# Gathering with an add into the output's place, and experts four tiles of keys earlier

## The chip, the cores and the metric

One core of a Trainium2 chip runs the kernel. The metric is the device time of one execution in microseconds (us), as the median of several runs. Lower is better.

## The reference

The input x holds 2 sequences of 2048 tokens of 128 numbers, 4096 tokens in all. Everything is float32. With xn = layernorm(x) the result is

```
s      = xn W_spin^T + b_spin
local  = softmax((s W_J^T) s^T / sqrt(128)) s        # per sequence, 2048 x 2048
attn   = tanh(beta * (s + mean(s) W_global^T + local))
logits = xn Wg^T + bg ; the two best of 16 experts, softmax over the two
moe    = sum over the two of weight * (gated(xn Wgu[e] + bgu[e]) Wd[e] + bd[e])
out    = x + attn + moe
```

Each token goes through exactly 2 of 16 experts, so the expert part works on 8192 (token, expert) pairs.

## The kernel before, in words

**Attention.** The 4096 tokens are split into 8 query blocks (k, `NSB`) of 512. Each block walks over the 16 key tiles (j, `TB`) of its sequence, which gives 128 steps i = 16k + j (`STEPS`). In a step TensorE makes the scores of one key tile against the block's 512 queries (`score`, 3 products of 128x128 by 128x512, lines 556 to 558, for a value is kept as a high and a low part), ScalarE takes the exponential (L921) and the high part (L932, `ph`), VectorE the low part (L1106, `pl`), and TensorE multiplies both with the key tile's rows (`values`, 3 products at the same lines) two steps later (`LAG`). The block that comes next needs a row of maxima before its first step: 16 products (`maxima`, L609), each reduced on VectorE (L1121), spread over the steps j = 0 to 11 of the block before (`maxima_at`), then `shifts` at j = 12 and `shift_row` at j = 13. After a block its sum is turned (`fields`, L717 and L718, in steps 16k + 24 and 16k + 26), divided (`combine`, L1142 and L1145) and squashed (`squash`, L959) into `field`.

**Routing and scatters.** VectorE and GpSimd work out for every token which slot of the expert list each of its two pairs has (`choose`, and `route` in pieces 4 to 12; `ROUTE_AT` says in which step a piece stands). When the first positions `posu` are there, GpSimd issues 64 indirect DMAs (L517, one for each of 32 token tiles and each of the two choices), which scatter token rows of 512 B into the DRAM table `slots_x`.

**Experts.** The steps stop at step `MOE_AT` = 76 and the experts' part takes the engines: 20 groups of 4 slot tiles are read from `slots_x` into `xy`, turned (`turn_slots`, L661; the first two groups in steps MOE_AT - 2 and MOE_AT - 1), multiplied (`gate_up`, `down`), and stored as 1 KB rows (high and low half) into the DRAM table `slots_y`. The scores of steps 76 to 79 are made inside this part. Its turned tiles use the PSUM banks of the maxima, so the maxima of the steps before have to be reduced first.

**The end.** After the last `slots_y` store GpSimd issues 64 indirect gathers (L547): for each block k of 4 token tiles 4 gathers of the first choice into `made` and 4 of the second into `gy`. VectorE, between its attention work, adds `gy` to `made` (`add_both`, L1279, 1024 elements a partition), adds the two halves (`add_parts`, L1284, 512), and adds `field` (`finish`, L1290, 512). The tokens x themselves are loaded by SyncE (`tokens_in`) into `xs` and added to `field` by VectorE (`add_x`, L1275, 512). SyncE stores the finished block. `made` has room for 4 blocks and `gy` for 2. For the last block the adds stand at the end of VectorE's program (L1397 to L1410), ahead of `combine(7, ...)`.

The order on every engine is written out by hand: each engine runs its list in order and waits on semaphores.

## Time and profile before

| | us |
|---|---|
| median of 3 runs | 362.93 (360.56 to 363.42) |
| profiled execution, own time | 362.15 |
| profiled execution, span from first to last instruction | 360.4 |
| TensorE busy in the span | 324.9 (90%) |
| VectorE busy | 309.9 (86%) |
| ScalarE busy | 256.8 (71%) |
| GpSimd busy | 203.7 (57%) |

The times of the rows below are microseconds from the start of the span. The profiled execution's own time is 1.75 us longer than its span. Matmuls overlap in the records: one of 512 columns is listed with 0.39 us, but the next begins 0.2265 us later when nothing holds it up. So TensorE's real work is counted in products and not in busy time.

### The profile page before, as it was taken

What the parts mean: (1) busy time and instruction counts of PE and PEld (TensorE: products, weight loads), DVE (VectorE), ACT (ScalarE), POOL (GpSimd) and SP (SyncE); (2) the same over time, 40 slices, a digit from 0 to 9 for tenths busy, and PEclk for the clock granted to TensorE, in tenths of its full rate; (3) what the DMA queues carried; (4) which work ended last, traced back from release to release, by engine and by line L of the source; (5) the groups of instructions that cost most, each with busy time, mean ns of one, the idle gap of its engine ahead of it and who ended that gap; (6) DMA issues with size and microseconds to landing.
All of it is one profiled execution on the core that took longest, in us unless ns stands there. A gap on an engine that the chain in (4) does not pass through costs nothing.

```text
span 360.4 us, 5972 instructions
## 1 busy us (share of the span) xinstructions
PE 324.9 (90%) x1778; PEld 271.9 (75%) x1779; DVE 309.9 (86%) x630; ACT 256.8 (71%) x509; POOL 203.7 (57%) x271
## 2 busy tenths in 40 slices
PE   1878999998999999999978999999899998989980
PEld 1666788776777778888768999999788786867750
DVE  5988979999978999999769999888878999987855
ACT  2754777876699797687646988888787586578751
POOL 4276851325777777777113444534137777777760
PEclk9978999999999999999999999999999999999996
DMA  5999710000111211212222877765543354555551
GB/s 148 325 332 340 282 35 0 1 31 7 51 51 54 80 46 53 90 51 82 74 87 75 241 222 229 235 207 178 178 117 107 104 164 123 131 145 133 133 126 34
DMA packets 41359, 45.97 MB, mean 128 GB/s; under 512 B 3770, under 2 KB 33082, under 8 KB 41330
## 3 DMA queue, kind: packets, MB, share of 16 engines
q1 hardware_dynamic: 36162, 32.94, 29.1%
q0 software_dynamic: 5168, 12.67, 12.4%
q8 instruction: 15, 0.25, 0.3%
q14 instruction: 14, 0.11, 0.1%
HBM read 23.46 MB, written 22.12 MB: 126 GB/s over the span
## 4 chain that ended last, share of the span: by engine, by line
PE 40%; DVE 22%; POOL 19%; issue 8%; ACT 5%; DMA 4%; POOLq 0%; SPq 0%; ACTq 0%; DVEq 0%
POOL made L547 9%; POOL gy L547 8%; PE PS L556 8%; PE PS L558 8%; PE PS L557 8%; DVE mx L1121 6%; DVE pl L1106 5%; PE PS L609 4%; PE PS L661 2%; PE PS L786 2%; PE PS L771 2%; DVE stats L1077 2%; DMA xy<-slots_x 1%; PE PS L788 1%; PE PS L791 1%
## 5 line engine op out<-in xcount | busy, mean ns | idle before, releaser
L921 ACT ACTIVATE PS<-PS 128x512 f32<-128x512 f32 x128 | 74.8, 585 | 42.8 <-PE PS L558 41.2
L1106 DVE TENSOR_TENSOR pl<-PS,ph 128x512 fp32r<-128x512 f32 x128 | 87.7, 685 | 14.1 <-ACT ph L932 13.5
L1121 DVE TENSOR_REDUCE mx<-PS 128x1 f32<-128x512 f32 x128 | 84.3, 682 | 6.0 <-PE PS L609 6.0
L932 ACT ACTIVATE ph<-PS 128x512 fp32r<-128x512 f32 x128 | 76.5, 598 | 12.1 <-PE PS L558 0.8
L517 POOL DMA_INDIRECT slots_x<-xn,posu x64 | 63.0, 985 | 19.7 <-issue 17.1
L609 PE MATMUL PS<-xT,gq 128*128 128x512 f32 x128 | 49.5, 423 | 6.6 <-DVE mx L1121 6.3
L556 PE MATMUL PS<-gq,xT 128*128 128x512 f32 x128 | 52.4, 410 | 1.5 <-ACT gq L937 0.8
L556 PE MATMUL PS<-ph,rows 128*128 128x512 f32 x128 | 51.5, 402 | 1.8 <-DVE pl L1106 1.8
L558 PE MATMUL PS<-gq,xT 128*128 128x512 f32 x128 | 50.1, 391 | 0.0
L558 PE MATMUL PS<-ph,rows 128*128 128x512 f32 x128 | 50.1, 391 | 0.0
L557 PE MATMUL PS<-pl,rows 128*128 128x512 f32 x128 | 50.0, 391 | 0.0
L557 PE MATMUL PS<-gq,xT 128*128 128x512 f32 x128 | 50.0, 390 | 0.0
L536 POOL TENSOR_TENSOR gu_sb<-gu_sb 128x512 f32<-128x512 f32 x20 | 25.9, 1293 | 40.9 <-DVE gu_sb L1353 40.9
L547 POOL DMA_INDIRECT made<-slots_y,posu x32 | 32.2, 1007 | 20.0 <-DMA slots_y<-yr 10.6
L609 PEld LDWEIGHTS PS<-xT,gq 128*128 128x128 f32 x128 | 24.5, 194 | 18.1 <-DVE mx L1121 13.2
L547 POOL DMA_INDIRECT gy<-slots_y,posu x32 | 32.2, 1006 | 9.8 <-issue 9.8
L556 PEld LDWEIGHTS PS<-ph,rows 128*128 128x128 f32 x128 | 24.1, 188 | 8.8 <-DVE pl L1106 4.7
L556 PEld LDWEIGHTS PS<-gq,xT 128*128 128x128 f32 x128 | 24.1, 189 | 6.0 <-DVE pl L1106 1.0
L1026 ACT ACTIVATE yr<-PS,w_slot 128x256 f32<-128x256 f32 x72 | 28.2, 488 | 0.0
L558 PEld LDWEIGHTS PS<-ph,rows 128*128 128x128 f32 x128 | 24.0, 188 | 5.3
L558 PEld LDWEIGHTS PS<-gq,xT 128*128 128x128 f32 x128 | 24.0, 188 | 5.3
L557 PEld LDWEIGHTS PS<-pl,rows 128*128 128x128 f32 x128 | 24.1, 188 | 4.4
(199 smaller groups left out, 682.8 us busy)
## 6 DMA issues: line engine op xcount, KB each, us to landing
slots_y<-yr SPq DMA_DIRECT2D x20, 512.0 KB, 3.1
slots_x<-xs SPq DMA_DIRECT2D x1, 5120.0 KB, 22.0
xy<-slots_x SPq DMA_DIRECT2D x20, 256.0 KB, 3.0
xn<-in_L_attn_x SPq DMA_DIRECT2D x8, 256.0 KB, 5.5
w_f<-in_L_ffn_Wgu SPq DMA_DIRECT2D x1, 2048.0 KB, 12.8
late<-in_L_ffn_Wgu SPq DMA_DIRECT2D x1, 2048.0 KB, 18.3
xs<-in_L_attn_x SPq DMA_DIRECT2D x8, 256.0 KB, 3.5
out_y<-made SPq DMA_DIRECT2D x7, 256.0 KB, 3.3
```

The costliest lines, as they stand in the source:

```text
L517: pool.indirect_dma_start(slots_x, bass.IndirectOffsetOnAxis(ap=posu[:, c, t:t + 1], axis=0), xn[:, t], None).then_inc(scat[c][0 if c else ...
L536: g.tensor_tensor(gu_sb[:, u, 1], gu_sb[:, u, 1], gu_sb[:, u, 0], ALU.mult).then_inc(au_ready, 1)
L547: pool.indirect_dma_start((made[:, k % 4], gy[:, k % 2])[c][:, t], None, slots_y, bass.IndirectOffsetOnAxis(ap=posu[:, c, 4 * k + t:4 * k ...
L556: mm(o, ah, bh, start=start, stop=False)
L557: mm(o, ah, bl, start=False, stop=False)
L558: return mm(o, al, bh, start=False, stop=stop)
L609: mm(o, gq[:, k % 3, 0, a * P:(a + 1) * P], xT[k // CB][:, 0, 512 * c:512 * c + 512], start=True, stop=True).then_inc(mx_fill, 1)
L921: A(S[:, n % 3], S[:, n % 3], ACT.Exp).then_inc(exp_done, 1)
L932: A(ph[:, i % RING], S[:, n % 3], ACT.Copy).then_inc(s_hi, 1)
L1026: ins = A(yr[:, u, 2 * h + a], O[:, h, 2 * D * a:2 * D * a + 2 * D], ACT.Copy, scale=w_slot[:, g, 2 * h + a:2 * h + a + 1])
L1106: v.tensor_tensor(dst, S[:, n % 3], high.bitcast(F32), ALU.subtract).then_inc(s_lo, 1)
L1121: v.tensor_reduce(mx4[:, a, c:c + 1], MX[:, n % 2], AX.X, ALU.max).then_inc(mx_free, 1)
```

## The change

- **Gathers.** All gathers write into `made` with an add (`compute_op=ALU.add`); `gy` is gone. Before them SyncE fills the place: the tokens x into the first half of each row and zeros (a new constant tile `zeros`) into the second half, two DMAs a block (`tokens_in`, semaphore `base_in`). Block k's first-choice gathers wait for these, its second-choice gathers wait until its first-choice ones have landed; between the two stand the first-choice gathers of the next block.
- **VectorE.** `add_x` and `add_both` are gone. `add_parts` stands at steps MOE_AT + 16 + 6k and `finish` at MOE_AT + 17 + 6k or 16k + 30, whichever is later. In the last block the halves are added per half, then come `combine`, and the final add.
- **Loads.** The base of block 0 is issued ahead of the last `slots_y` store, those of blocks 1 to 3 behind it, that of block k + 4 when block k's store has landed. The earlier loads into `xs` are gone from SyncE's list.
- **Experts at step 72.** `MOE_AT` is 72. 8 of the 16 maxima of block 5 come before the experts' part (j = 0 to 5) and 8 behind it (two in each of the steps 72 to 75). The fields of block 3 (steps 72 and 74) fall behind the experts' part.
- **Routing.** Pieces 4 to 12 stand at steps 16, 17 (5, 6 and 7 together), 18, 19, 21, 24 and 25 instead of one each at 16 to 20 and 22 to 25.

```diff
@@ -37,7 +37,7 @@
     BIG = 3.0e38
     LAG = 2
     RING = 4
-    MOE_AT = 5 * TB - 4
+    MOE_AT = 5 * TB - 8
@@ -77,8 +77,7 @@
         (late,), (rows1,) = over((("late", [P, 2 * TB * D], F32),), (("rows1", [P, 2, TB, D], F32R),))
-        (yr, gy), (rows0,) = over((("yr", [P, 2, 4, 2 * D], F32), ("gy", [P, 2, 4, 2 * D], F32)),
-                                  (("rows0", [P, 2, TB, D], F32R),))
+        (yr,), (rows0,) = over((("yr", [P, 2, 4, 2 * D], F32),), (("rows0", [P, 2, TB, D], F32R),))
         rows = [rows0, rows1]
         gq = sb("gq", [P, 3, 2, 512], F32R)
         sl = sb("sl", [P, NT, AC])
@@ -89,7 +88,7 @@
         (_, w_f), (w2,) = over((("w_pad", [P, NE, WC], F32), ("w_f", [P, NE, WC], F32)), (("w2", [P, 2, NE, WC], F32R),))
         wh, wl = w2[:, 0], w2[:, 1]
         wb = sb("wb", [P, 2, 512], F32R)
-        xs = sb("xs", [P, 2, 4, D])
+        zeros, oh_place = sb("zeros", [P, 4, D]), sb("oh_place", [P, NT * NE // 2])
         oT, oT_part = sb("oT", [P, 512]), sb("oT_part", [P, 512])
         b_rows = sb("b_rows", [NSLOT_TILES, 2, D], F32R)
         bd_hl = [b_rows[0:NE, 0], b_rows[0:NE, 1]]
@@ -130,7 +129,7 @@
         cols_of = sb("cols_of", [1, NG, 4], I32)
         b_st = th[0:NE, 0:WC]
-        ohb = xs[:, 1].rearrange("p a d -> p (a d)").bitcast(BF16)[:, 0:NT * NE]
+        ohb = oh_place[:].bitcast(BF16)
         mean_bc = wglT
         wgu0 = late[:].rearrange("p (e n) -> p e n", e=NE)
@@ -190,7 +189,8 @@
         th_ready, au_ready, y_ready, y_last = sem("th_ready"), sem("au_ready"), sem("y_ready"), sem("y_last")
         gat = [sem(f"gat{k}") for k in range(NSB - 1)]
         gat_last, gat_half = sem("gat_last"), [sem("gat_half0"), sem("gat_half1")]
-        x_added, both_added, parts_added, fin_ready = sem("x_added"), sem("both_added"), sem("parts_added"), sem("fin_ready")
+        base_in = [sem(f"base_in{k}") for k in range(NSB)]
+        parts_added, fin_ready = sem("parts_added"), sem("fin_ready")
         stored = [sem(f"stored{k}") for k in range(NSB)]
@@ -250,8 +250,13 @@
         def mx_no(k, q):
             return k * 17 + q
-        def maxima_at(j):
+        def maxima_at(i):
+            j, m = i % TB, MOE_AT % TB
+            if i // TB == MOE_AT // TB and j >= m - 2:
+                first = -(-4 * (m - 2) // 3) + 2 * (j - m)
+                return range(first, min(first + 2, 16)) if j >= m else ()
             return range(-(-4 * j // 3), -(-4 * (j + 1) // 3)) if j < 12 else ()
@@ -298,7 +303,7 @@
                 sp.wait_ge(consts, 10)
                 sp.dma_start(
                     slots_x.rearrange("(p r) d -> p (r d)", p=P).rearrange("p (a n) -> p a n", n=4 * D),
-                    bc(xs[:, 0].rearrange("p a d -> p (a d)"), [P, NSLOT_TILES // 4, 4 * D], 1)).then_inc(zeroed, 16)
+                    bc(zeros[:].rearrange("p a d -> p (a d)"), [P, NSLOT_TILES // 4, 4 * D], 1)).then_inc(zeroed, 16)
                 sp.wait_ge(b_one, 1)
                 sp.wait_ge(wfold, 4)
@@ -308,20 +313,14 @@
                 sp.dma_start(b_d.rearrange("e (s n) -> e s n", s=2), b_rows[0:NE].bitcast(F32)).then_inc(bd_kept, 16)
                 def tokens_in(k):
-                    if k >= 2:
-                        sp.wait_ge(x_added, k - 1)
-                    sp.dma_start(xs[:, k % 2], x_v[k // CB][:, 4 * (k % CB):4 * (k % CB) + 4]).then_inc(ld_x[k], 16)
-                sp.wait_ge(zeroed, 16)
-                tokens_in(0)
-                sp.wait_ge(e_fill, e_no["R", 1] + 1)
-                tokens_in(1)
+                    sp.dma_start(made[:, k % 4, :, 0:D], x_v[k // CB][:, 4 * (k % CB):4 * (k % CB) + 4]).then_inc(base_in[k], 16)
+                    sp.dma_start(made[:, k % 4, :, D:2 * D], zeros[:]).then_inc(base_in[k], 16)
                 sp.wait_ge(eid_ready, 1)
                 sp.dma_start(eid_d, eid[0:NSLOT_TILES]).then_inc(eid_kept, 16)
                 sp.wait_ge(eid_kept, 16)
                 sp.dma_start(cols_of[:], eid_d.rearrange("(o g a) z -> o g (a z)", o=1, a=4)).then_inc(cols_in, 16)
-                tokens_in(2)
-                tokens_in(3)
                 sp.wait_ge(b_found, 16)
                 sp.dma_start(b_slots.rearrange("s (t n) -> t s n", t=NSLOT_TILES), b_rows[:].bitcast(F32)).then_inc(b_kept, 16)
@@ -334,7 +333,6 @@
                 sp.wait_ge(wb_clear, 1)
                 bias_in(0, 0)
                 bias_in(1, 1)
-                tokens_in(4)
                 for s in scat[0]:
                     sp.wait_ge(s, 16 * NT // 4)
                 sp.wait_ge(scat[1][0], 16 * NT)
@@ -366,20 +364,25 @@
                     results_out(2 * j + 1, 1)
                     bias_in(2 * j + 1, 1)
                 for g in range(NG - 4, NG + 2):
+                    if g == NG + 1:
+                        sp.wait_ge(t_fill, gated_fill(NG - 1) + 1)
+                        tokens_in(0)
                     results_out(g, g % 2)
                     if g < NG:
                         bias_in(g, g % 2)
-                tokens_in(5)
-                tokens_in(6)
+                for k in range(1, 4):
+                    tokens_in(k)
                 for k in range(NSB):
-                    if k == 4:
-                        tokens_in(7)
                     for h in range(2 if k == NSB - 1 else 1):
                         t = 4 * (k % CB) + 2 * h
                         n = 2 if k == NSB - 1 else 4
                         sp.wait_ge(fin_ready, k + 1 + h)
                         sp.dma_start(out_v[k // CB][:, t:t + n], made[:, k % 4, 2 * h:2 * h + n, 0:D]).then_inc(stored[k], 16)
+                    if k + 4 < NSB:
+                        sp.wait_ge(stored[k], 16)
+                        tokens_in(k + 4)
                 for k in range(NSB):
                     sp.wait_ge(stored[k], 32 if k == NSB - 1 else 16)
@@ -400,7 +403,7 @@
             g.memset(onesb[:], 1.0).then_inc(consts, 1)
             g.memset(onesr[:].bitcast(F32), 1.0).then_inc(consts, 1)
             g.iota(iot[:], [[1, NSLOT_TILES]], base=0, channel_multiplier=0).then_inc(consts, 1)
-            g.memset(xs[:, 0], 0.0).then_inc(consts, 1)
+            g.memset(zeros[:], 0.0).then_inc(consts, 1)
             g.memset(nmz[:], 0.0).then_inc(consts, 1)
             g.memset(AE[:, :, D:D + 2], 0.0).then_inc(consts, 1)
             pool.wait_ge(consts, 12)
@@ -537,16 +540,23 @@
             pool.wait_ge(y_out[0], 16 * (NG // 2))
             pool.wait_ge(y_out[1], 16 * (NG // 2))
-            for k in range(NSB):
-                for c in range(2):
-                    if c and k >= 2:
-                        pool.wait_ge(both_added, k - 1)
-                    if c == 0 and k >= 4:
-                        pool.wait_ge(stored[k - 4], 16)
-                    for t in range(4):
-                        pool.indirect_dma_start((made[:, k % 4], gy[:, k % 2])[c][:, t], None, slots_y,
-                                                bass.IndirectOffsetOnAxis(ap=posu[:, c, 4 * k + t:4 * k + t + 1], axis=0)
-                                                ).then_inc(gat[k] if k < 7 else (gat_last, gat_half[t // 2])[c], 16)
+            def gather(k, c):
+                if c:
+                    pool.wait_ge(gat[k] if k < NSB - 1 else gat_last, 64)
+                else:
+                    pool.wait_ge(base_in[k], 32)
+                for t in range(4):
+                    pool.indirect_dma_start(made[:, k % 4, t], None, slots_y,
+                                            bass.IndirectOffsetOnAxis(ap=posu[:, c, 4 * k + t:4 * k + t + 1], axis=0),
+                                            compute_op=ALU.add
+                                            ).then_inc(gat[k] if k < NSB - 1 else (gat_last, gat_half[t // 2])[c], 16)
+            gather(0, 0)
+            for k in range(1, NSB):
+                gather(k, 0)
+                gather(k - 1, 1)
+            gather(NSB - 1, 1)
         @block.tensor
         def _(pe):
@@ -727,7 +737,7 @@
                 if query_at(i):
                     queries(query_at(i))
                 if k + 1 < NSB:
-                    for q in maxima_at(j):
+                    for q in maxima_at(i):
                         maxima(k + 1, q, q // 4, q % 4)
                     if j == 13:
                         shift_row(k + 1)
@@ -735,7 +745,7 @@
                     values(i - LAG)
                 if i in (MOE_AT - 2, MOE_AT - 1):
-                    pe.wait_ge(mx_free, 16 * (MOE_AT // TB + 1) + 15 + i % 2)
+                    pe.wait_ge(mx_free, 16 * (MOE_AT // TB + 1) + -(-4 * (MOE_AT % TB - 2) // 3) - 1 + i % 2)
                     turn_slots(i % 2, 1 - i % 2, i % 2 + 1)
                 for use in SPIN_AT.get(i, ()):
                     spins_and_logits(*use)
@@ -820,7 +830,7 @@
             gate_up(0, columns[0])
             pe.wait_ge(t_lo, rows_fill(1) + 1)
             turn_slots(0, 0, 3)
-            pe.wait_ge(e_free, e_no["F", 3, 1] + 1)
+            pe.wait_ge(e_free, e_no["F", 2, 1] + 1)
             columns[1] = experts_of(1)
             expert_step(1, columns, results=False)
             for g in range(2, NG):
@@ -1262,37 +1272,25 @@
                     v.tensor_copy(small[:, 0], small[:, 1]).then_inc(route_done, 1)
             CHOOSE_AT = {7: (0, 0), 9: (0, 1), 10: (0, 2), 11: (0, 3), 12: (1, 0), 13: (1, 1), 14: (1, 2), 15: (1, 3)}
-            ROUTE_AT = {16: 4, 17: 5, 18: 6, 19: 7, 20: 8, 22: 9, 23: 10, 24: 11, 25: 12}
+            ROUTE_AT = {16: (4,), 17: (5, 6, 7), 18: (8,), 19: (9,), 21: (10,), 24: (11,), 25: (12,)}
             def slot_lo(n, bank, pair):
                 dve.wait_ge(t_hi, n + 1)
                 v.tensor_tensor(pair[1], tiles4(T[:, bank]), pair[0].bitcast(F32), ALU.subtract).then_inc(t_lo, 1)
-            def add_x(k):
-                dve.wait_ge(ld_x[k], 32)
-                dve.wait_ge(tanh_ready, k + 1)
-                f = field[:, 4 * k:4 * k + 4]
-                v.tensor_tensor(f, f, xs[:, k % 2], ALU.add).then_inc(x_added, 1)
-            def add_both(k):
+            def add_parts(k):
                 dve.wait_ge(gat[k], 128)
-                v.tensor_tensor(made[:, k % 4], made[:, k % 4], gy[:, k % 2], ALU.add).then_inc(both_added, 1)
-            def add_parts(k):
-                dve.wait_ge(both_added, k + 1)
                 m = made[:, k % 4]
                 v.tensor_tensor(m[:, :, 0:D], m[:, :, 0:D], m[:, :, D:2 * D], ALU.add).then_inc(parts_added, 1)
             def finish(k):
                 dve.wait_ge(parts_added, k + 1)
-                dve.wait_ge(x_added, k + 1)
+                dve.wait_ge(tanh_ready, k + 1)
                 m = made[:, k % 4, :, 0:D]
                 v.tensor_tensor(m, m, field[:, 4 * k:4 * k + 4], ALU.add).then_inc(fin_ready, 1)
-            ADD_X_AT = {40: 0, 54: 1, 66: 2, 78: 3, 94: 4, 110: 5, 126: 6}
-            BOTH_AT = {MOE_AT + 11 + 6 * k: k for k in range(7)}
-            PARTS_AT = {MOE_AT + 12 + 6 * k: k for k in range(7)}
-            FINISH_AT = {MOE_AT + 13 + 6 * k + 2 * (k == 6): k for k in range(7)}
+            PARTS_AT = {MOE_AT + 16 + 6 * k: k for k in range(7 if MOE_AT < 76 else 6)}
+            FINISH_AT = {max(MOE_AT + 17 + 6 * k, TB * k + 30): k for k in PARTS_AT.values()}
             def step(i):
                 k, j = divmod(i, TB)
@@ -1305,7 +1303,7 @@
                     if query_at(i - 1):
                         queries_lo(query_at(i - 1))
                 if k + 1 < NSB:
-                    for q in maxima_at(j):
+                    for q in maxima_at(i):
                         maximum(k + 1, q, q // 4, q % 4)
                     if j == 12:
                         shifts(k + 1)
@@ -1317,8 +1315,8 @@
                     global_in(GLOBAL_AT[i - 1])
                 if i in CHOOSE_AT:
                     choose(*CHOOSE_AT[i])
-                if i in ROUTE_AT:
-                    route(ROUTE_AT[i])
+                for piece in ROUTE_AT.get(i, ()):
+                    route(piece)
                 if i in ROW_LO_AT:
                     c = ROW_LO_AT[i]
                     t = 4 * c
@@ -1328,10 +1326,6 @@
                 for n in WEIGHT_LO_AT.get(i, ()):
                     dve.wait_ge(w_hi, n + 1)
                     v.tensor_tensor(wl[:, n], w_f[:, n], wh[:, n].bitcast(F32), ALU.subtract).then_inc(w_lo, 1)
-                if i in ADD_X_AT:
-                    add_x(ADD_X_AT[i])
-                if i in BOTH_AT:
-                    add_both(BOTH_AT[i])
                 if i in PARTS_AT:
                     add_parts(PARTS_AT[i])
                 if i in FINISH_AT:
@@ -1393,17 +1387,18 @@
             for i in range(MOE_AT, STEPS):
                 step(i)
             prob_lo(STEPS - 1)
-            dve.wait_ge(gat_last, 64)
+            for k in range(len(FINISH_AT), NSB - 1):
+                add_parts(k)
+                finish(k)
+            m = made[:, 3]
             for h in range(2):
+                t = slice(2 * h, 2 * h + 2)
                 dve.wait_ge(gat_half[h], 32)
-            dve.wait_ge(ld_x[7], 32)
-            m = made[:, 3]
-            link(v.tensor_tensor(m, m, gy[:, 1], ALU.add))
-            link(v.tensor_tensor(m[:, :, 0:D], m[:, :, 0:D], m[:, :, D:2 * D], ALU.add))
-            link(v.tensor_tensor(m[:, :, 0:D], m[:, :, 0:D], xs[:, 1], ALU.add))
+                v.tensor_tensor(m[:, t, 0:D], m[:, t, 0:D], m[:, t, D:2 * D], ALU.add).then_inc(parts_added, 1)
             combine(7, 0)
             combine(7, 1)
+            dve.wait_ge(parts_added, NSB + 1)
             for h in range(2):
                 t = slice(2 * h, 2 * h + 2)
                 dve.wait_ge(tanh_ready, NSB + h)
```

## Rows read from the trace of the kernel before

**Rows 1.** The page's chain that ended last, by line, as shares of the span.

```profile
POOL made L547 9%; POOL gy L547 8%; PE PS L556 8%; PE PS L558 8%; PE PS L557 8%; DVE mx L1121 6%; DVE pl L1106 5%; PE PS L609 4%; PE PS L661 2%; PE PS L786 2%; PE PS L771 2%; DVE stats L1077 2%; DMA xy<-slots_x 1%; PE PS L788 1%; PE PS L791 1%
```

**Rows 2.** The chain in order of time, its last transfer: start, duration, what.

```profile
348.69 3.84 DMA gy<-slots_y,posu
```

**Rows 3.** Timeline of VectorE (DVE): start, duration, instruction [idle before <- releaser].

```profile
81.00 1.09 DVE L1244 TENSOR_TENSOR late<-PS,late 128x512 f32<-128x512 f32 x1
...
85.91 0.18 DVE L1252 CAST posu<-mk 128x32 uint32<-128x32 f32 x1
...
262.85 0.69 DVE L1275 TENSOR_TENSOR sl<-sl,xs 128x512 f32<-128x512 f32 x1 [1.16 <-ACT sl L959]
...
280.80 0.68 DVE L1284 TENSOR_TENSOR made<-made 128x512 f32<-128x512 f32 x1
...
352.71 1.23 DVE L1402 TENSOR_TENSOR made<-made,gy 128x1024 f32<-128x1024 f32 x1 [4.62 <-DMA gy<-slots_y,posu]
...
355.43 0.17 DVE L1142 RECIPROCAL rden<-PS 128x2 f32<-128x2 f32 x1
```

**Rows 4.** Timeline of TensorE (PE), same columns.

```profile
169.62 0.39 PE L556 MATMUL PS<-gq,xT 128*128 128x512 f32 x1
...
173.03 0.39 PE L556 MATMUL PS<-gq,xT 128*128 128x512 f32 x1
...
179.12 0.66 PE L661 MATMUL PS<-ident,xy 128*128 128x128 f32 x4 [0.50 <-DVE mx L1121]
...
182.92 0.66 PE L661 MATMUL PS<-ident,xy 128*128 128x128 f32 x4 [1.10 <-DVE mx L1121]
...
184.80 0.28 PE L556 MATMUL PS<-w,ph 128*128 x1
...
349.64 1.13 PE L718 MATMUL PS<-AE,oT 128*128 128x130 f32 x8 [0.52 <-issue]
```

**Rows 5.** Windows behind the experts: busy us (x instructions) by engine, clock, DMA share, GB/s.

```profile
266.00:296.00 30.00, 29.50 (x140) 24.30 (x139) 27.64 (x49) 21.05 (x37) 22.96 (x24) 1.00 0.40 111
296.00:326.00 30.00, 27.96 (x125) 21.61 (x124) 27.11 (x47) 20.52 (x36) 23.29 (x23) 1.00 0.52 139
326.00:352.00 26.00, 23.63 (x107) 18.11 (x105) 17.24 (x30) 18.42 (x33) 18.16 (x19) 1.00 0.53 132
```

**Rows 6.** Line 547, all gathers: duration in ns, idle time before, landing.

```profile
L547 POOL DMA_INDIRECT made<-slots_y,posu x32: 952/957/1541, 266.0 to 343.5; - x32
...
issue: 19.2, 63
...
DMA to landing us min/median/max: 2.7/2.8/5.1
```

**Rows 7.** Timeline of GpSimd (POOL): routing, first and last scatter, weights, first gather.

```profile
75.43 1.29 POOL L487 TENSOR_TENSOR late<-late 128x512 f32<-128x512 f32 x1 [2.23 <-DVE late L1230]
...
82.38 1.26 POOL L492 TENSOR_TENSOR late<-late 128x512 f32<-128x512 f32 x1 [1.49 <-DVE late L1247]
...
87.19 1.23 POOL L517 DMA_INDIRECT slots_x<-xn,posu  x1 [0.66 <-POOL xn L514]
...
128.68 1.14 POOL L502 DMA_INDIRECT b_rows<-b_d,eid_u  x1 [0.31 <-issue]
...
171.69 0.96 POOL L517 DMA_INDIRECT slots_x<-xn,posu  x1 [0.30 <-issue]
176.88 0.19 POOL L524 COPY w_slot<-xy 128x4 f32<-128x4 f32 x1 [4.23 <-DMA xy<-slots_x]
...
177.69 0.19 POOL L524 COPY w_slot<-xy 128x4 f32<-128x4 f32 x1 [0.46 <-DMA xy<-slots_x]
...
266.03 1.04 POOL L547 DMA_INDIRECT made<-slots_y,posu  x1 [10.57 <-DMA slots_y<-yr]
```

**Rows 8.** DMA view of 266 to 352 us: packets, MB, share of the 16 engines.

```profile
q0 software_dynamic: 3070, 8.39, 37.3%
q1 hardware_dynamic: 4053, 2.47, 10.5%
```

## The prediction, made blind

> **What bounds the kernel now.** I read first the chain that ended last, because it says which work, if shorter, makes the kernel shorter. By line [rows 1] the gathers stand at its head with 9% and 8% of the span: once the experts are done, the whole rest of the kernel is on the chain as GpSimd issuing gather after gather. The chain in order of time [rows 2] shows the last one issued at 348.69 and landed at 348.69 + 3.84 = 352.53. VectorE had then been idle for 4.62 us [rows 3], and began the adds of the last block at 352.71; `combine(7, 0)` began at 355.43. From there to the end of the span are 360.40 - 355.43 = 4.97 us (combine, squash, add, store).
>
> The next question is who is second. TensorE's last eight narrow products start at 349.64 and end at 350.77 [rows 4]; the first four, which `combine(7, 0)` needs, are done at about 350.2. So without the gathers `combine(7, 0)` could have begun at 350.3, and the attention work is only 5.13 us behind the gathers. That is the most that a change of the gathers alone can bring.
>
> The third view is the windows behind the experts [rows 5]. From 266 to 350.77 TensorE runs 372 products. By the program 48 of them are narrow (40 of L717 and L718, 8 of L616), some 0.1 us each (0.36 us for the four between 174.61 and 174.97 in the same timeline, which I round up), and 324 are wide at 0.2265 us: 73.4 + 4.8 = 78.2 us of 84.8. So TensorE stands still for 6.6 us of the end. It does so where VectorE is full: in 266 to 326 VectorE is busy for 54.75 of 60 us, and TensorE's waits name VectorE's `pl` and `mx`.
>
> **The experts earlier.** Step 70 begins at 169.62 [rows 4]. In the changed order it holds three scores, three values and then `turn_slots`, so 6 x 0.2265 = 1.36 us later, at 170.98, TensorE wants the first turned tile's source. When is it there? Before, the last scatter was issued at 171.69, and the weights were taken from `xy` at 176.88 and 177.69 [rows 7]; the tile can be turned about 0.4 us after that, at 177.3 and 178.1. In the changed kernel all this moves with the routing.
>
> The routing is a ping-pong between VectorE and GpSimd. Now piece 5's result starts GpSimd's L487 at 75.43 as before, but pieces 6 and 7 follow at once (seven small instructions, 0.2 us each), so GpSimd can begin L490 when L487 ends (76.7) and ends it at 77.9. VectorE takes piece 8, 1.09 us long [rows 3], behind one low part and one maximum at about 78.0 and not at 81.0; L492 then runs 79.4 to 80.7 and not from 82.38 [rows 7]; piece 9 comes behind step 19's low part and two maxima, at 81.2, and `posu` at 82.1 and not at 86.1 [rows 3]. The first scatter starts 4.0 us earlier than 87.19. The scatters are one unbroken row of issues, so the last one, and the tiles, also come 4.0 us earlier: first tile at 173.3, second at 174.1. TensorE wants the first at 170.98 and so waits 2.3 us; it takes 0.45 for the four turns, 1.36 for step 71, 0.45 and 1.36 for the second tile and the two late values, and starts the experts at about 177.0. Before they started at 184.80 [rows 4], and before them TensorE waited 1.9 us for maxima (178.46 to 179.12 and 181.67 to 182.92), a wait that goes, since no maxima stand in steps 70 and 71. Net cost for TensorE 2.3 - 1.9 = +0.4 us. Bounds: -1.9 (the tiles come in time) and +4.4 (the routing isn't earlier at all). TensorE's other work is only moved: 4 steps, 8 maxima and 2 fields from ahead of the experts to behind them. The first gather goes from 266.03 to 266.03 - 7.8 = 258.2.
>
> **The gathers.** 64 issues of 0.96 us with 0.30 us between them [rows 6]; in all 352.53 - 266.03 = 86.5 us from first issue to last landing. If an issue costs the same, the last one lands at 258.2 + 86.5 = 344.7. What an adding issue costs no row shows. The nearest rows: an issue that writes DRAM from SBUF in 512 B rows takes the same 0.96 us as one that reads 1 KB rows, so bytes and direction don't count; and one with 80 rows instead of 128, L502, took 1.14 us [rows 7], so even 48 descriptor pairs fewer bought nothing. Against it: all 0.96 us could be work per row, and the operand that is read a second time could double it. So the cost is between 0 and +0.96 us an issue; I take 0, by the row with 80. A gain below nothing is excluded: the add asks for everything that the plain gather does.
>
> The new wait of block k's second-choice gathers for its first-choice ones: 4 gathers stand between, 4 x 1.26 + 0.30 = 5.4 us, and a landing takes 2.8 us, at most 5.1 [rows 6]. Hidden; queued behind the wait are all later gathers, so if landings took over 5.4 us each excess would be paid up to 8 times. The waits for `base_in`: block 0's loads are issued some 3 us ahead of the last `slots_y` store, behind which GpSimd waits anyway; block k + 4 needs that block k is stored. `add_parts` of block 0 stood at step 88 and ran at 280.80 [rows 3], and it stands there again; its gathers have landed by 258.2 + 12 x 1.26 + 2.8 = 276.1, so VectorE doesn't wait; the store is out at some 286, the base in at some 290, and the gathers of block 4 (the 29th issue) start at 258.2 + 28 x 1.26 = 293.5. Six steps take 10 us and eight gathers too, so the margins of 3 to 4 us hold. SyncE's two more issues ahead of the last `slots_y` store (0.4 us each) end before its data are ready.
>
> **VectorE.** Gone are 7 `add_x` of 0.69 us, 4 of them behind the experts [rows 3], and 7 `add_both` of 1.23 us, all behind them: 8.6 + 2.8 = 11.4 us of the end. Moved there are 8 maxima, 4 low parts and a field, but with them comes TensorE work of the same steps, so the load per step falls. TensorE's 6.6 us of standstill are all that this can return; a part of them is the latency at the fields and the last steps, where VectorE is idle. I take 2.6 us, bounds 0 and 6.6. In front of the experts three `add_x` go (2.1 us) and the bunched routing pieces delay one low part by 1.3 us; TensorE runs full there, and I set both against each other at 0 (bounds -1 and +1). In the last block the adds of 2.72 us [rows 3] become two of 0.42 us per half, ahead of `combine`.
>
> **The sum.** Attention chain: 350.3 for `combine(7, 0)`, + 0.4 - 2.6 = 348.1. Gather chain: 344.7 + 0.45 (add of the last half) = 345.2. The later one is attention, by 2.9 us, so the end is 348.1 + 4.97 = 353.1 us of span, and with the 1.75 us around it 354.8; I forecast 355.0 us. Against the profiled execution's own 362.15 that is -7.1 us or -2.0%. That execution is 0.8 us below the median of the runs shown, so against 362.93 it is -2.2%. Less than about 1% can't be told from no change by a measurement of this kernel. The forecast's own range: the best is set by the gathers, 344.7 + 0.45 + 4.97 + 1.75 = 351.9, or 351.0 if the tiles are ready in time; the worst with the VectorE bound at 0 and +1 in front is 358.4.
>
> **Where page and rows differ.** The rows say nothing of an add within a DMA, and I let an issue keep its length. The Trainium skill speaks against the change. Its page "GPSIMD Engine Reference" (section "When to use GPSIMD") says that a pair of cores generates the descriptors, one those that read and the other those that write; its page "Collectives: The Full Stack" (section "The bandwidth ceiling: the fold count and why AG ≠ RS ≠ AR") says that a reducing transfer has two read descriptors where a copy has one, and runs at about half the rate for this reason. By these two the reading list doubles, in making and in moving; no run here has shown it. What that would do as a mechanism of this kernel is worked out from rows in the first two rivals.
>
> **Rivals.**
> - *The adding issue is longer, and the gathers bind harder (slower).* Place: the 64 issues in a row. The point from which it decides: the gathers may end 2.9 us later for nothing, 0.045 us an issue; the kernel is slower than before from (360.4 - 4.97 - 0.45 - 344.7) / 64 = 0.16 us an issue. If a quarter to a half of 0.96 us is added (0.24 to 0.48), the last landing is at 360.1 to 375.4 and the time 367 to 383 us; I name 372. For it: nothing else than issuing fills the gap from one gather to the next. Against it: the 80 rows at 1.14 us. Chance 0.23.
> - *The DMA engines are the new bound.* The gathers use 37.3% of the engines in 86 us, 32 us in all or 0.50 us each; SyncE's 2.47 MB cost 9.0 us, 3.7 us per MB [rows 8]. Twice that for a gather is 64 us, and 2 MB of stores, 2 of tokens and 2 of zeros 23 us: 87 us of engines in the 84 us that the gathers have. Landings stretch over 5.4 us, the second-choice gathers wait for the first, and at 0.7 us a block that is 5.6 us: last landing 350 to 352, time 357 to 359; I name 358. Chance 0.12.
> - *The scatters don't come earlier*, since pieces 8 and 9 wait for GpSimd all the same, VectorE's order is disturbed, or the tiles come late for another reason: the change doesn't do what it says. TensorE then waits 4 us more at step 70: 358.8, I name 359. Chance 0.07.
> - The forecast: 0.58.
>
> **How the numbers follow.** The predicted time is the likeliest case, 355.0. The range must hold 0.8: the forecast's own (351.0 to 358.4), the second and the third rival to 361, and the shortest part of the first, so that it ends at 364. Faster by over 1% (below 359.3): 0.58, 0.09 of the second and 0.04 of the third, 0.71. Within 1%: the rest of both, and an issue that is 0.1 to 0.2 us longer, 0.08. Slower: 0.21.
>
> **What would show it.** Right: the first gather near 258; gathers 1.26 us apart; experts' first product near 177 with a wait of 2 us for GpSimd ahead of the first turn; VectorE no longer idle ahead of the last block for DMA, and the chain's end on TensorE and VectorE; landings under 5 us. Wrong: adding issues over 1.0 us (first rival); a wait of L547 on its own DMAs, or VectorE waiting at `add_parts` (second); the first scatter at 87 (third). The number is wrong most easily by the return of TensorE's standstill, which I only took a share of.

## The result, and the profile after

The changed kernel takes 390.69 us (median of 4 runs, 389.14 to 391.4) against 362.87 us before (median of 4 runs, 360.56 to 363.42): the ratio is 1.077, its 95% interval 1.073 to 1.081. The forecast was 355.0 us with a range to 364; the change is slower by 27.8 us. Only the first rival pointed this way, and its dearest case was 383. The profiled execution has a span of 389.7 us in an own time of 391.4.

The page of the changed kernel shows the chain that ended last, by engine and by line (to compare with [rows 1]), and the gathers' group.

```profile
POOL 41%; PE 23%; DVE 15%; issue 12%; DMA 5%; ACT 2%; SPq 0%; POOLq 0%; ACTq 0%; DVEq 0%
POOL made L550 24%; POOL slots_x L520 16%; PE PS L566 4%; PE PS L567 4%; PE PS L568 4%; DVE mx L1131 3%; DVE pl L1116 2%; DMA xy<-slots_x 2%; PE PS L796 2%; PE PS L671 2%; PE PS L781 2%; PE PS L619 1%; DVE stats L1087 1%; PE PS L798 1%; PE PS L801 1%
...
L550 POOL DMA_INDIRECT made<-slots_y,posu x64 | 99.5, 1554 | 30.4 <-issue 19.2
```

The gathers are 24% of the chain where both groups together were 17%, and one takes 1554 ns. The view of their line says the same in more detail (to compare with [rows 6], where the middle number was 957 ns).

```profile
L550 POOL DMA_INDIRECT made<-slots_y,posu x64: 1542/1551/1629, 262.4 to 379.5; - x64
its engine sat idle before it (us, times) until:
  issue: 19.2, 63
  DMA slots_y<-yr: 11.2, 1
who waited for it (us, times):
  DVE made L1284: 26.4, 6
  DVE made L1398: 0.9, 1
...
DMA to landing us min/median/max: 3.7/3.9/5.8
```

All 64 are longer, none below 1542 ns. The first one, with no other gather under way, took 1.63 us, so an adding issue isn't long because it waits for earlier gathers. The 63 pauses are 19.2 / 63 = 0.30 us each, as before; the only other wait is the one at the start. So neither the wait of the second-choice gathers for the first-choice ones nor the wait for the base loads ever held GpSimd. The whole stretch is issue after issue.

The two spans part as follows, each term from first and last rows of the gathers and the end of the span. The first gather is at 262.40 and not 266.03: -3.6 us. From the start of the first to the start of the last are 379.50 - 262.40 = 117.1 us and not 82.7: +34.4. What lies behind the start of the last one is 389.7 - 379.5 = 10.2 us and not 11.7: -1.5. Together +29.3, the difference of the spans.

Where does the rest of the kernel stand? The windows behind the experts (to compare with [rows 5]: busy us by engine, granted clock, DMA share, GB/s):

```profile
266.00:296.00 30.00, 29.59 (x142) 24.50 (x142) 24.06 (x45) 21.59 (x38) 24.92 (x17) 1.00 0.60 94
296.00:326.00 30.00, 22.25 (x91) 17.32 (x90) 17.84 (x31) 14.93 (x27) 25.13 (x17) 0.94 0.74 135
326.00:356.00 30.00, 22.64 (x91) 17.68 (x90) 14.05 (x26) 16.67 (x30) 25.13 (x17) 0.89 0.66 110
356.00:382.00 26.00, 17.90 (x68) 13.79 (x66) 10.61 (x21) 12.07 (x21) 21.09 (x14) 0.87 0.60 91
```

In the first window TensorE is fuller than before and VectorE has 3.6 us less to do: the `add_x` and `add_both` are gone. From the second on, TensorE runs two thirds as many products (91 against 142), while GpSimd never has a pause but the 0.30 us. The waits of 255 to 390 us say how the one gets to the other:

```profile
DVE made L1284 <- DMA made<-slots_y,posu: 26.4, 6, 6.0
...
PE PS L566 <- DVE pl L1116: 18.1, 6, 5.4
```

`add_parts` stands in VectorE's queue ahead of the next `pl`. VectorE waits there six times for gathers, and TensorE waits behind it for `pl`. The attention work is no second bound here: it is held back by the gathers, block by block. TensorE's granted clock was 0.94 to 0.87 in these windows and 1.00 in the one where it ran full.

The end, in the timeline of VectorE (to compare with the last lines of [rows 3]): the last half waits 0.92 us for its gathers, and then `combine` waits another 0.58 us for TensorE's last fields, which the gathers had held back too.

```profile
383.53 0.43 DVE L1398 TENSOR_TENSOR made<-made 128x256 f32<-128x256 f32 x1 [0.92 <-DMA made<-slots_y,posu]
384.54 0.17 DVE L1152 RECIPROCAL rden<-PS 128x2 f32<-128x2 f32 x1 [0.58 <-PE PS L728]
```

### The profile page after: what moved, and what is told of

It reads as the page before. It is cut to its first block, busy times and chain, and to the rows that moved or that the text cites. A ratio compares the mean times of both kernels' runs of the same rounds, so it can differ in the third digit from the quotient of the medians.

```text
span 389.7 us, 5955 instructions
## 1 busy us (share of the span) xinstructions
PE 335.7 (86%) x1779; PEld 280.0 (72%) x1779; DVE 298.3 (77%) x615; ACT 257.0 (66%) x509; POOL 238.8 (61%) x271
## 4 chain that ended last, share of the span: by engine, by line
POOL 41%; PE 23%; DVE 15%; issue 12%; DMA 5%; ACT 2%; SPq 0%; POOLq 0%; ACTq 0%; DVEq 0%
POOL made L550 24%; POOL slots_x L520 16%; PE PS L566 4%; PE PS L567 4%; PE PS L568 4%; DVE mx L1131 3%; DVE pl L1116 2%; DMA xy<-slots_x 2%; PE PS L796 2%; PE PS L671 2%; PE PS L781 2%; PE PS L619 1%; DVE stats L1087 1%; PE PS L798 1%; PE PS L801 1%
## 5 line engine op out<-in xcount | busy, mean ns | idle before, releaser
L550 POOL DMA_INDIRECT made<-slots_y,posu x64 | 99.5, 1554 | 30.4 <-issue 19.2
L1116 DVE TENSOR_TENSOR pl<-PS,ph 128x512 fp32r<-128x512 f32 x128 | 87.5, 685 | 27.0 <-ACT ph L942 26.5
L942 ACT ACTIVATE ph<-PS 128x512 fp32r<-128x512 f32 x128 | 76.5, 598 | 11.8 <-PE PS L568 0.4
L566 PE MATMUL PS<-ph,rows 128*128 128x512 f32 x128 | 53.3, 416 | 18.4 <-DVE pl L1116 18.3
L566 PE MATMUL PS<-gq,xT 128*128 128x512 f32 x128 | 53.6, 418 | 1.5 <-ACT gq L947 0.8
L568 PE MATMUL PS<-gq,xT 128*128 128x512 f32 x128 | 51.3, 401 | 0.0
L567 PE MATMUL PS<-pl,rows 128*128 128x512 f32 x128 | 51.3, 401 | 0.0
L568 PE MATMUL PS<-ph,rows 128*128 128x512 f32 x128 | 51.3, 401 | 0.0
L567 PE MATMUL PS<-gq,xT 128*128 128x512 f32 x128 | 51.2, 400 | 0.0
L566 PEld LDWEIGHTS PS<-ph,rows 128*128 128x128 f32 x128 | 25.0, 195 | 26.2 <-DVE pl L1116 16.3
L566 PEld LDWEIGHTS PS<-gq,xT 128*128 128x128 f32 x128 | 25.0, 195 | 6.3 <-DVE pl L1116 1.0
L568 PEld LDWEIGHTS PS<-ph,rows 128*128 128x128 f32 x128 | 24.8, 193 | 5.6
L568 PEld LDWEIGHTS PS<-gq,xT 128*128 128x128 f32 x128 | 24.7, 193 | 5.5
L567 PEld LDWEIGHTS PS<-pl,rows 128*128 128x128 f32 x128 | 25.1, 196 | 4.8
L1279 DVE TENSOR_TENSOR pl<-PS,ph 128x512 fp32r<-128x512 f32 x40 | 25.8, 681 | 3.2 <-ACT ph L957 2.7
```

The lines of the kernel that those rows point to most:

```text
L550: pool.indirect_dma_start(made[:, k % 4, t], None, slots_y, bass.IndirectOffsetOnAxis(ap=posu[:, c, 4 * k + t:4 * k + t + 1], axis=0), com ...
L566: mm(o, ah, bh, start=start, stop=False)
L567: mm(o, ah, bl, start=False, stop=False)
L568: return mm(o, al, bh, start=False, stop=stop)
L942: A(ph[:, i % RING], S[:, n % 3], ACT.Copy).then_inc(s_hi, 1)
L1116: v.tensor_tensor(dst, S[:, n % 3], high.bitcast(F32), ALU.subtract).then_inc(s_lo, 1)
```

## The experiments

The theory after the result (theory A) is that the adding issue itself is longer, and that this is the whole loss. The rivals: the doubled reading fills the DMA engines, and the longer issue only goes with it (B); the new order of experts, routing and maxima costs time of its own (C).

**The forms of the issue.** One kernel gives each output block another form of gather: number of rows, bytes of a row, with and without the add. Its output is therefore not the reference's.

```
rows_n, add, width = {0: (128, 1, 2 * D), 1: (64, 1, 2 * D), 2: (128, 0, 2 * D), 3: (64, 0, 2 * D),
                      4: (128, 1, D), 5: (64, 1, D), 6: (16, 1, 2 * D), 7: (16, 0, 2 * D)}[k]
```

> A measurement of the issue itself: the changed kernel in which the 8 gathers of each block have another form: block 0 128 rows of 1 KB with add, 1 64 rows with add, 2 128 rows plain, 3 64 rows plain, 4 128 rows of 512 B with add, 5 64 rows of 512 B with add, 6 16 rows with add, 7 16 rows plain; the output lacks what the forms leave out. Theory, that the add costs work per row (a second read per row to describe): 1.55, 1.26, 0.96, about 0.96 (as the 80 rows of line 502 said), then 1.55 and 1.26 again for 512 B, 1.03 for 16 rows with add. Rival, a fixed price of an adding issue: 1.55 in blocks 0, 1, 4, 5 and 6. Rival, that an issue's length is bytes: block 4 shorter than block 0.

One row of each form from the timeline of GpSimd, in the order of the blocks 0 to 7 (start, duration):

```profile
333.25 1.56 POOL L554 DMA_INDIRECT made<-slots_y,posu  x1 [0.30 <-issue]
...
340.58 1.43 POOL L554 DMA_INDIRECT made<-slots_y,posu  x1 [0.30 <-issue]
...
355.77 0.95 POOL L554 DMA_INDIRECT made<-slots_y,posu  x1 [0.30 <-issue]
...
367.64 0.90 POOL L554 DMA_INDIRECT made<-slots_y,posu  x1 [0.30 <-issue]
...
378.84 1.54 POOL L554 DMA_INDIRECT made<-slots_y,posu  x1 [0.30 <-issue]
...
390.94 1.41 POOL L554 DMA_INDIRECT made<-slots_y,posu  x1 [0.30 <-issue]
...
403.38 1.31 POOL L554 DMA_INDIRECT made<-slots_y,posu  x1 [0.30 <-issue]
...
417.94 0.84 POOL L554 DMA_INDIRECT made<-slots_y,posu  x1 [0.30 <-issue]
```

Plain: 0.95, 0.90 and 0.84 us for 128, 64 and 16 rows, so 0.11 us for 112 rows: 1.0 ns a row, and 0.82 us whatever the rows. Adding: 1.56, 1.43, 1.31, so 2.2 ns a row and 1.27 us whatever the rows. Half the bytes change next to nothing (1.54 and 1.41). Of the 0.6 us that the add costs at 128 rows, 0.45 is a surcharge whatever the rows and 0.15 the doubled price of a row. None of the three forecasts held as it stood: the price isn't all in the rows (1.26 us was forecast for 64), it isn't all fixed (1.55 for 16), and it isn't in the bytes. The lines come from one execution, of 442.63 us; the other issues of each form differ from the line shown by 0.07 us at most, but for one of 16 rows with 1.78 us. What GpSimd does in the 0.45 us no trace shows.

**Order, gathers, both: a first measurement.** Together with this kernel stood the order alone (experts from step 72, routing in five steps, maxima split), the adding gathers alone, and the changed kernel with plain gathers. A plain gather overwrites the tokens and the first choice, so they are missing from that one's output. The edits stand with the second measurement of the same kernels, below.

> The change's order (experts at step 72, routing in five steps, maxima split) with the gathers, the buffer gy and VectorE's adds of the kernel before. My theory, that the whole loss is the length of an adding issue: first gather near 262.4 as in the changed kernel, gathers 1.26 us apart, last landing near 262.4 + 86.5 = 348.9, then 2.7 us of adds and 4.97 us to the end: span 356.6, time 358.4 us (-1.2%). Rival, that the order itself costs (TensorE's wait for the first tile, disturbed routing): 363 us or more.

> The adding gathers alone, with experts at step 76, maxima and routing as before. Theory (64 issues at 1.855 us, the order worth the 3.6 us by which the first gather came earlier): first gather near 266, last landing near 387, time 394.3 us. Rival, that the order is worth nothing or costs: 390.7 us or less.

> The changed kernel with plain gathers in the place of adding ones, everything else (base loads, waits between a block's two gathers, order, VectorE's list) kept; the output then lacks the tokens and the first choice. Theory, that only the issue with the add is long: issues of 0.96 us, last landing near 348.9, then 0.45 + 4.97: span 354.3, time 356 us. Rival, that the waits between the gathers of a block or the base loads on the DMA engines cost too: issues 0.96 us but gaps ahead of the second-choice gathers, time over 362 us.

Every kernel of this measurement, the one before too, was some 100 us longer than elsewhere (before: 465.4 us median, 456 to 475). Between 96 and 178 us TensorE, ScalarE and VectorE mostly stood still (TensorE was busy for 19 of these 82 us) while GpSimd's scatters went on; the chain of the order alone names no instruction for six pieces of 7 to 14 us there, and for six more of 2 to 9 us between 346 and 423 us. Three of the first six are

```profile
134.77 14.46 another core or an unknown queue
150.52 9.91 another core or an unknown queue
161.04 14.09 another core or an unknown queue
```

In the changed kernel with plain gathers GpSimd moreover waited for the base loads, the very gaps that its rival named:

```profile
its engine sat idle before it (us, times) until:
  DMA made<-zeros: 34.8, 3
```

The medians, 469.1, 468.7 and 472.5 us, say nothing on the change, since such stretches set them. Durations of single issues agree with those elsewhere: 0.96 us without the add and 1.55 with it. What caused the stretches I did not find. For all times that follow the kernel before was measured again, with 364.02 us beside the plain gathers, the fill, the order alone and its early tail, and 362.29 us beside the others.

**Plain gathers in the changed kernel.** Tokens and first choice are missing from the output again.

```
-                                            ...axis=0),
-                                            compute_op=ALU.add
+                                            ...axis=0)
```

> The changed kernel with plain gathers instead of adding ones, all else kept (the output lacks tokens and first choice). Theory: issues of 0.96 us, last landing near 348.9, time 356 us. Rival, that the waits between a block's gathers or the base loads cost: gaps ahead of second-choice gathers, time over 362 us.

358.56 us, ratio 0.986 (0.981 to 0.991); span of the profile 355.4. One argument of one instruction is some 32 us. No gather waits for a base load or for another gather here, so the gaps of the first measurement aren't a property of the program. The rest of the forecast can now be seen on its own: gathers, then TensorE's windows, then the end of the attention work, which does bind here.

```profile
342.89 1.15 POOL L550 DMA_INDIRECT made<-slots_y,posu  x1 [0.30 <-issue]
```

```profile
266.00:296.00 30.00, 29.83 (x142) 24.63 (x141) 24.02 (x44) 21.60 (x39) 22.99 (x24) 1.00 0.47 131
296.00:326.00 30.00, 29.67 (x137) 24.27 (x136) 26.13 (x48) 22.53 (x39) 22.99 (x24) 1.00 0.62 172
```

```profile
349.67 1.13 PE L727 MATMUL PS<-AE,oT 128*128 128x130 f32 x8 [0.52 <-issue]
```

TensorE misses 0.5 us of 60 where it missed 2.5 before [rows 5], and its last fields come at 349.67, after the last gather has landed (VectorE adds its last half from 348.05 on without a wait).

**Plain gathers, with the time put back.** To part A from B the same kernel gets a fill of a spare tile behind every gather: the length of the adding issue without its second reading. The output lacks the same parts.

```
+                    if filled:
+                        pool.wait_ge(fill_done, len(filled))
+                    g.memset(fill[:], 0.0).then_inc(fill_done, 1)
+                    filled.append(t)
```

> As the one before, with a memset of a scratch tile on GpSimd behind each plain gather, which brings the distance from gather to gather to about 1.8 us without an add in the DMA (the output lacks the same). Theory, that the length of the issue is what the add costs, and the doubled reading by the DMA engines nothing: the time of the changed kernel, 386 to 391 us for a distance of 1.80 to 1.86 us. Rival, that a part of the loss is the DMA engines' work: clearly less, by over 3 us, than the distance alone gives (first gather + 64 distances + 10 us).

383.96 us, 1.057 (1.053 to 1.062). Gather and fill stand like this:

```profile
369.30 0.97 POOL L554 DMA_INDIRECT made<-slots_y,posu  x1 [0.16 <-issue]
370.27 0.62 POOL L559 MEMSET fill<- 128x600 f32 x1
371.04 0.96 POOL L554 DMA_INDIRECT made<-slots_y,posu  x1 [0.16 <-issue]
```

With the first gather at 261.36 the distance is (371.04 - 261.36) / 63 = 1.741 us, less than the 1.80 to 1.86 intended, and between 1.31 (0.96 + 0.30 and some longer ones) and the change's 117.1 / 63 = 1.859. The end of the two kernels isn't a fair measure, since another wait stands there in this one:

```profile
373.84 0.42 DVE L1405 TENSOR_TENSOR made<-made 128x256 f32<-128x256 f32 x1 [0.38 <-DMA made<-slots_y,posu]
375.39 0.17 DVE L1159 RECIPROCAL rden<-PS 128x2 f32<-128x2 f32 x1 [1.12 <-PE PS L735]
```

So I compare from the first gather to the add that follows the last landing: 373.84 - 261.36 = 112.5 us here, 383.53 - 262.40 = 121.1 in the change, 8.7 more. The distances alone account for 63 x (1.859 - 1.741) = 7.4. The other 1.2 us are the last landing, 4.0 us behind its issue in the change and 2.8 here, paid once at the end. That is the most that B can have of the loss of 28 us. It is not that the second reading isn't there. In the DMA view of the gathers' stretch (packets, MB, share of 16 engines) the change has

```profile
q0 software_dynamic: 8928, 8.13, 48.8%
q1 hardware_dynamic: 12071, 6.26, 18.2%
```

and this kernel, in 117 us, has

```profile
q0 software_dynamic: 3072, 8.39, 27.6%
```

so 0.488 x 122 / 62 = 0.96 us of the engines for an adding gather (the stretch of 122 us ends before the transfers of the last two, 8.13 MB of 8.39) against 0.276 x 117 / 64 = 0.50 for a plain one. The Trainium skill's page "Collectives: The Full Stack" (section "The bandwidth ceiling: the fold count and why AG ≠ RS ≠ AR") gives a reducing transfer two read descriptors; the engines' time agrees, at 1.9 times. The packets don't show it as plainly: they are 144 a gather and not 48, three times as many. But both queues together fill 67% of the engines, because the issues come too slowly to fill them.

**The adding gathers alone**, in the order of before (the changed kernel with `MOE_AT`, `maxima_at`, two waits that go with them and `ROUTE_AT` put back; two of the edits are shown):

```
-    MOE_AT = 5 * TB - 8
+    MOE_AT = 5 * TB - 4
-            ROUTE_AT = {16: (4,), 17: (5, 6, 7), 18: (8,), 19: (9,), 21: (10,), 24: (11,), 25: (12,)}
+            ROUTE_AT = {16: 4, 17: 5, 18: 6, 19: 7, 20: 8, 22: 9, 23: 10, 24: 11, 25: 12}
```

> The adding gathers alone in the old order (experts at 76, routing as before). Theory: first gather near 266, 63 distances of 1.859 us, 4.0 us of landing and 6.2 us behind it, span 393.3, time 394.5 us, 1.010 of the changed kernel. Rival, that the order is worth nothing: 390.7 us or less.

394.24 us, 1.091 (1.084 to 1.098), as the theory said. Against the whole change the order gives back 3.6 us by the medians, and by the ratios (1.091 against 1.077, of 363) 5.1, with intervals of about 3. Its first gather is at 265.74, so by the two profiles the order brings it 3.3 us forward; but start-up differs between executions by some 3 us (GpSimd's add of the result of piece 5 begins at 74.56 to 77.68 us in the profiles outside the first measurement), and counted from that add it is 190.9 us against 184.8, 6.1 us. Where the gathers bind, the order is worth 3 to 6 us.

**The order alone** (theory C), the reverse of that edit made in the kernel before, with no block's `finish` earlier than step 16k + 30:

> The change's order alone (experts at 72, five-step routing) with plain gathers, gy and VectorE's adds as before. Theory, that the length of an adding issue is all of the loss: last landing near 348.9, time 358.4 us. Rival, that the order costs by itself: 363 us or more.

365.43 us, 1.004 (1.000 to 1.008). The forecast of a gain of 5 to 6 us is missed. Its windows and its end:

```profile
266.00:296.00 30.00, 28.87 (x134) 22.88 (x134) 26.44 (x47) 20.63 (x36) 23.30 (x23) 1.00 0.38 110
296.00:326.00 30.00, 29.32 (x128) 22.39 (x129) 28.02 (x50) 20.57 (x36) 23.12 (x23) 1.00 0.53 140
```

```profile
356.04 0.50 PE L560 MATMUL PS<-ph,rows 128*128 128x512 f32 x1 [1.04 <-DVE pl L1110]
...
358.21 1.13 PE L722 MATMUL PS<-AE,oT 128*128 128x130 f32 x8 [0.52 <-issue]
```

The last gather is issued at 347.55, and nobody waits for its landing; TensorE's last fields come at 358.21 and not 349.64 [rows 4], and `combine` follows the last of VectorE's adds at 359.20 without a pause. Moved behind the experts without VectorE's relief, the maxima and low parts bind there. C is wrong as a cause of the loss (0.4%), but the order alone isn't a gain either: of its two forecasts the rival's came.

**VectorE's relief alone**: the order of before, plain gathers into the output's place, no adds of tokens and first choice (both edits shown above, in the changed kernel). Those parts are missing from the output.

> Experts at 76 and routing as before, VectorE's list, base loads and waits of the changed kernel, but plain gathers (the output lacks tokens and first choice): what VectorE's relief is worth in the old order. Theory, that the gathers bind there: first gather 266.0 + 86.5 + 0.45 + 4.97 us, time 359.7 us, so 1.1 us over the same with experts at 72 (358.6). Rival, that the order was worthless altogether: 358.6 us or less.

358.88 us, 0.992 (0.988 to 0.996), the same within the intervals as with the order (0.986, 0.981 to 0.991), and too near to both forecasts to choose between them. That the gathers bind here is told by the profile: the fields are done early and VectorE waits 2.6 us for the last half.

```profile
346.67 1.13 PE L723 MATMUL PS<-AE,oT 128*128 128x130 f32 x8 [0.52 <-issue]
```

```profile
348.73 0.96 POOL L546 DMA_INDIRECT made<-slots_y,posu  x1 [0.30 <-issue]
```

**The five-step routing alone**, experts from step 76:

> The kernel before with the five-step routing alone, experts at step 76. Theory (the first tile isn't what step 74 waits for, and the pieces only change places): within 0.3% of before. Rival, that the bunched routing is what disturbs the new order: 1 us or more slower.

363.59 us, 1.004 (1.000 to 1.008), where within 0.3% was forecast; the interval holds both. The first scatter comes at 83.95. Counted again from GpSimd's add of piece 5's result (75.43 before [rows 7], 75.35 here), it is 8.6 us to the first scatter and not 11.8, so 3.2 us less and not 4.0. With the experts where they were, nobody wants the tiles earlier.

**An early tail in the order alone, and in the kernel before.** In the last block the tokens' and first-choice adds are made ahead of the last half's arrival, so that two short adds are left behind it (the added lines are shown).

```
+            link(v.tensor_tensor(m[:, :, 0:D], m[:, :, 0:D], m[:, :, D:2 * D], ALU.add))
+            for h in range(2):
+                t = slice(2 * h, 2 * h + 2)
+                dve.wait_ge(gat_half[h], 32)
+                link(v.tensor_tensor(m[:, t, 0:D], m[:, t, 0:D], y[:, t, 0:D], ALU.add))
+                link(v.tensor_tensor(m[:, t, 0:D], m[:, t, 0:D], y[:, t, D:2 * D], ALU.add))
```

> The order alone, and in the last block the tokens and the two halves of the first choice are added when the first choice has landed, so that only two half-width adds per half (0.42 us each) stand behind the last landing instead of 2.7 us. Theory (the gathers still bind): 1.8 us faster than the order alone, 356.6 us. Rival, that attention binds at the end: no difference from the order alone.

> The kernel before, in whose last block the tokens and the halves of the first choice are added as soon as the first choice has landed; behind the last landing stand 0.42 us adds instead of 2.72 us. Theory (in the old order the gathers bind the end and VectorE is idle for 4.6 us ahead of these adds): 1.3 to 1.9 us faster than before, ratio 0.995 to 0.996. Rival, that attention binds as in the new order: no difference.

With the new order 364.89 us (1.003, interval 0.998 to 1.008), not told from 365.43: VectorE came to these adds only when the gathers had landed, and `combine` (358.02) again followed its last add without a pause. In the kernel before 362.76 us (10 runs, 1.000, interval 0.997 to 1.004). There its profile does show the intended thing at the end,

```profile
354.74 0.43 DVE L1405 TENSOR_TENSOR made<-made,gy 128x256 f32<-128x256 f32 x1 [1.99 <-DMA gy<-slots_y,posu]
355.20 0.43 DVE L1406 TENSOR_TENSOR made<-made,gy 128x256 f32<-128x256 f32 x1
355.66 0.17 DVE L1142 RECIPROCAL rden<-PS 128x2 f32<-128x2 f32 x1
```

`combine` 0.92 us behind the wait's end and not 2.72 [rows 3]. Why the median of the times shows no gain of 1.8 us is open; in the one profile start-up took 2.2 us more (the first gather is at 267.72, 1.7 us late), and from VectorE's last add to the end of the span it took 3.8 us and not 2.4. This last stretch is 2.4 to 2.6 us in seven of the ten profiles outside the first measurement and 3.8 to 4.3 in three (this one, the fill and VectorE's relief), without a cause that I found; single runs of both kernels spread over some 4 us.

## Why the prediction was wrong

**The step that failed: "What an adding issue costs ... I take 0, by the row with 80".** Measured +0.59 us, between the bounds of 0 and 0.96. The row with 80 rows showed that rows are cheap. From it I concluded that a second list of descriptors is cheap, and so that the kind of the issue doesn't count. The rows are cheap (1.0 ns, or 2.2 with the add); the kind costs 0.45 us whatever the rows. The row was a poor witness besides: its issue of 1.14 us took 0.94 in every other profile but one. The first rival had the mechanism, its place and its point of decision (0.16 us an issue) right, and took at most half of 0.96 where it was 0.6 of it. The bound of +0.96 that I had worked out held, but my range ended at an issue longer by some 0.2 us.

In the profile's span the miss is 389.7 - 353.1 = 36.6 us, and its parts are these. From the first to the last issue it took 34.4 us longer than before: 0.55 us a distance and not 0.59, for some issues before had been longer than 0.96 us too. The first gather was at 262.40 and not 258.2, 4.2 us. Behind the start of the last issue stood 10.2 us and not 3.84 + 0.45 + 4.97 = 9.3, 0.9 us. From these 39.6 go the 3.0 us by which the gathers could end later for nothing. That the forecast's own sum with 0.59 put in gives 344.7 + 37.8 = 382.5 for the last landing and 389.7 for the time, near the 390.69 measured, is in part luck: it has 3.4 us too much for the issues and 4.2 too little ahead of them.

**The doubled reading**, that I had weighed against the row and left out of the sum, was there: the price per row and the engines' time both about double (2.2 and 1.9 times). Three quarters of the longer issue (0.45 of 0.6 us) are no price per row, though.

**The second rival** (DMA engines) had the doubling right too, 0.96 x 64 = 61 us of engines against 64, but its wait never came, since slower issues also space the transfers. I had named VectorE's wait at `add_parts` as its sign; that wait came, 26.4 us of it, from late issues. A sign that two rivals share tells nothing.

**The experts earlier: mechanism right, sized too well.** TensorE waited 2.27 us at the first turn (forecast 2.3), and only 0.26 us more ahead of the experts. Counted from piece 5's add (77.61 in the change, which began 2.2 us late), the experts begin after 102.9 us, where the forecast's 177.0 - 75.43 is 101.6 and before it was 109.4. Of the 1.3 us, 0.8 are the routing. In the changed kernel with plain gathers it was 104.1 and in the order alone 105.2, so the term of 7.8 us was 4.2 to 6.5. Of the 4.2 us by which the first gather came late, 2.2 are the start-up, 1.3 this term, and 0.7 the experts' part itself.

About 1.1 us of the spread is TensorE's clock, which the forecast had not priced. Behind the wait for the first tile, in the changed kernel with plain gathers:

```profile
173.36 0.63 PE L670 MATMUL PS<-ident,xy 128*128 128x128 f32 x4 [2.26 <-POOL xy L529]
...
174.06 0.39 PE L566 MATMUL PS<-gq,xT 128*128 128x512 f32 x1
...
175.29 0.63 PE L567 MATMUL PS<-ph,rows 128*128 128x512 f32 x1
```

One product is listed with 0.63 us where it was 0.39. From 174.6 to 178.0 the granted clock is 0.50, the lower of its two levels (1.2 GHz and not 2.4), and products follow each other after 0.43 us and not 0.23. Ahead of it TensorE had stood still for 2.3 us and then run for 1.2. From the first turn to the experts it took 5.3 us in all four profiles that show this (plain gathers, the fill, the order alone and its early tail), and 4.2 in the changed kernel, where the clock stayed at 1.00 behind the same wait. Why it stayed there is open.

**VectorE's relief: a hit in the sum, in part by luck.** From the experts' first product to the last fields TensorE took 164.8 us before. The forecast puts 8.2 us of moved work in and takes 2.6 off: 170.4. The plain kernel has 349.67 - 178.63 = 171.0. The two terms apart are both larger and their errors cancel: the order alone needs 358.21 - 182.84 = 175.4 (+10.5), and the relief returns 4.3 of it; without the order the relief returns 3.8 (346.67 - 185.67 = 161.0).

**The tail.** The last adds took 0.43 us and `combine` began 1.0 us behind the landing of the last half, 0.58 of it a wait for the fields; 389.7 - 384.54 = 5.2 us remain, forecast 4.97.

**Without the failed step** the forecast was 355.0 and the kernel with plain gathers takes 358.56, or 98.6% of the one before where I said 97.8%: 3 us; the experts' term is 2.5 us short there (104.1 against 101.6).

## What to carry to other kernels

An option on a DMA that GpSimd issues can change the price of the issue itself. Where the issues stand in an unbroken row, multiply an unknown price by their count before anything else: 63 x 0.55 us outweighed all that the engines saved. Bound such a price by its kind, not by its size: a cheap row of another length of the same kind says nothing of another kind. And three edits that unload one engine and load the next have to be priced as a set: the order alone (+0.4%), the relief alone (-0.8%) and both (-1.4%), each within about 0.4 to 0.5%, aren't a sum of prices found one by one: in the first VectorE's list set the end, in the second the gathers, in the third the attention work. No version that computes all of the output came out faster than the kernel before.

## What the runs showed of the hardware

- An indirect DMA's issue on GpSimd, fitted through 16, 64 and 128 rows: 0.82 us + 1.0 ns a row plain, 1.27 us + 2.2 ns a row with an add, nearly the same for rows of 512 B as of 1 KB (measured with the add), and 0.30 us between two. A plain gather of 128 x 1 KB takes 0.50 us of the 16 DMA engines, an adding one 0.96; it lands after 3.9 us at the median and not 2.8.
- Behind a wait of 2.2 to 2.6 us TensorE ran at the lower level of its clock for 3.1 to 3.5 us in four profiles, which cost 1.1 us each time, and in one it did not.
- A small integer operation on VectorE took 1.15 us, where such operations beside it took 0.17, while GpSimd's 1.29 us long `late` add from 77.61 ran, and ended with it:

```profile
77.57 0.17 DVE L1243 TENSOR_SCALAR tiles_i<-late 128x16 int32<-128x16 f32 x1
77.78 1.15 DVE L1244 TENSOR_SCALAR tiles_i<-tiles_i 128x16 int32<-128x16 int32 x1
78.96 0.17 DVE L1245 CAST late<-tiles_i 128x16 f32<-128x16 int32 x1
```

  It took 1.15 or 1.16 us in all nine profiles of kernels with the five-step routing, where it falls beside that add, and 0.17 in all five of kernels with the routing of before, where it begins after the add has ended.
- In one measurement all kernels were some 100 us longer. In the profile of the order alone the first gather came 70 us later than in the same kernel elsewhere, after standstills beside the scatters with nothing in the trace that released them.
